# More sparse tiles at the end of a GroupNorm and patch top-k kernel, and dense stores that wait for sparse patches

## The reference, cut to what matters

```python
# x: (4, 256, 256, 256) float32
y = group_norm(x, groups=32)                     # (x - mean) / sqrt(var + 1e-5)
s = 0.5 * (|horizontal [-1,0,1] gradient of y| + |vertical gradient of y|) + 0.5 * |y|
sp = s averaged over patches of 32 x 32          # (4, 256 channels, 64 patches)
mask = rank of sp among the 256 channels < 128   # for each image and each patch position
out = x + y * mask
```

## Time and profile before

| | us |
|---|---|
| median of 3 runs (2054.36 to 2056.93) | 2055.26 |
| the profiled execution, its own time | 2053.4 |
| its span in the trace | 2051.6 |

### The profile page before, as it was taken

How to read it: one execution, slowest core, us unless ns; L and a number is a source line. 1 busy time by engine, 2 the same in 40 slices (tenths; PEclk the granted TensorE clock), 3 DMA queues, 4 the chain that set the end, 5 groups by cost and what they waited for, 6 DMA issues and landing times.

```text
span 2051.6 us, 16270 instructions
## 1 busy us (share of the span) xinstructions
PE 1373.3 (67%) x3528; PEld 674.0 (33%) x3528; DVE 1537.1 (75%) x2113; ACT 1593.2 (78%) x2405; POOL 1402.4 (68%) x975
## 2 busy tenths in 40 slices
PE   5899899786777777777767776877677777600000
PEld 2444444333333333433333333433333333300000
DVE  7988887888778787899787878888877787652210
ACT  4999999897898889998888898898888988730123
POOL 7999999677676667767766676767666766531226
PEclk9999999888988888988888888989888888855555
DMA  5898775199999999999999999999999999699995
GB/s 246 338 358 338 305 317 206 62 368 428 429 430 433 433 429 431 404 383 422 430 431 435 427 432 431 383 396 423 432 432 429 432 432 425 251 382 428 425 423 178
DMA packets 53672, 780.53 MB, mean 380 GB/s; under 512 B 11175, under 2 KB 11175, under 8 KB 16240
## 3 DMA queue, kind: packets, MB, share of 16 engines
q1 hardware_dynamic: 42096, 759.19, 88.1%
q0 software_dynamic: 11520, 20.77, 2.8%
HBM read 532.68 MB, written 293.60 MB: 403 GB/s over the span
## 4 chain that ended last, share of the span: by engine, by line
DMA 44%; ACT 16%; issue 11%; PE 8%; DVE 7%; another core or an unknown queue 6%; POOL 3%; DVEq 2%; SPq 1%; ACTq 1%; POOLq 0%
DMA again<-in_x_dram 41%; ACT again L706 8%; PE vertical L610 4%; PE vertical L612 4%; ACT thrown L764 3%; DVE stats L807 3%; DMA out_dram<-ring,pair 2%; DVEq L798 2%; ACT vertical L758 2%; ACT ring L724 1%; DVE largest L1000 1%; DMA ring<-in_x_dram 1%; SPq L464 1%; DVE vertical L821 1%
## 5 line engine op out<-in xcount | busy, mean ns | idle before, releaser
L610 PE MATMUL vertical<-ring,plus 128*128 128x512 f32 (+1 forms) x1200 | 667.1, 641 | 304.5 <-ACT vertical L758 304.0
L299 POOL TENSOR_TENSOR pair<-ring 128x960 f32<-128x960 f32 x360 | 638.2, 1793 | 30.5 <-DVE scratch L978 21.9
L612 PE MATMUL vertical<-ring,minus 128*128 128x512 f32 (+1 forms) x1200 | 633.3, 612 | 0.0
L807 DVE BATCH_NORM_STATS2 stats<-ring 128x6 f32<-128x512 f32 x960 | 582.2, 677 | 25.5 <-DMA ring<-in_x_dram 14.9
L764 ACT ACTIVATE thrown<-ring,record 128x1024 bf16<-128x1024 f32 x480 | 548.2, 1142 | 8.8
L706 ACT ACTIVATE again<-again,coef 128x1024 f32<-128x1024 f32 x360 | 416.1, 1227 | 165.7 <-DMA again<-in_x_dram 165.7
L834 DVE TENSOR_REDUCE sums<-pair 128x2 f32<-128x1920 f32 (+1 forms) x212 | 454.8, 2145 | 84.7 <-POOL pair L299 84.0
L305 POOL TENSOR_TENSOR pair<-ring 128x960 f32<-128x960 f32 x120 | 269.3, 2244 | 296.2 <-DVE sums L834 272.0
L610 PEld LDWEIGHTS vertical<-ring,plus 128*128 128x128 f32 x1200 | 240.7, 212 | 578.2 <-ACT vertical L758 364.9
L612 PEld LDWEIGHTS vertical<-ring,minus 128*128 128x128 f32 x1200 | 250.7, 209 | 296.2 <-issue 296.2
L758 ACT ACTIVATE vertical<-vertical 128x960 f32<-128x960 f32 x320 | 303.6, 949 | 24.7 <-PE vertical L612 24.7
(11 more groups left out here) (108 smaller groups left out, 1245.0 us busy)
## 6 DMA issues: line engine op xcount, KB each, us to landing
ring<-in_x_dram SPq DMA_DIRECT2D x59, 4096.0 KB, 23.3
again<-in_x_dram SPq DMA_DIRECT2D x98, 2048.0 KB, 15.5
out_dram<-again SPq DMA_DIRECT2D x98, 2048.0 KB, 14.9
out_dram<-kept SPq DMA_DIRECT2D x12, 2048.0 KB, 11.3
kept<-in_x_dram SPq DMA_DIRECT2D x4, 4096.0 KB, 23.5
out_dram<-ring SPq DMA_DIRECT2D x6, 2048.0 KB, 32.7
kept<-in_x_dram SPq DMA_DIRECT2D x4, 2048.0 KB, 26.5
ring<-in_x_dram SPq DMA_DIRECT2D x4, 2048.0 KB, 28.0
```

Source lines behind the costliest of these rows:

```text
L299: return nc.gpsimd.tensor_tensor(part.rearrange("p (r c) -> p r c", r=PATCH), xs[:, w, :, 2:], xs[:, w, :, 0:PATCH - 2], ALU.subtract)
L610: nc.tensor.matmul(v[:, first:end], plus[:], xs[:, first + 2 * PATCH:end + 2 * PATCH], start=True, stop=False)
L612: done = nc.tensor.matmul(v[:, first:end], minus[:], xs[:, first:end], start=False, stop=True)
L807: nc.vector.bn_stats(stats[:, k, :], buffer[:, k * BN:(k + 1) * BN])
```

## The change

Sparse tiles become 4 to 13 (ten) in place of 8 to 13 (six): five pairs instead of three. Dense halves become 12 (tiles 15, 14, 0 to 3) in place of 20. The loop of image 0 copies tiles 4 to 9 where it copied 8 to 13; tiles 10 to 13 are copied by four new calls, one behind each of the four `load_ahead` calls after the loop. Each dense store but the first has a second wait: store n is issued only after ACT has finished 6n sparse patch columns.

```diff
-SPARSE_FIRST, SPARSE_END = 8, LAST - 1
+SPARSE_FIRST, SPARSE_END = 4, LAST - 1
...
-assert SPARSE_PAIRS[0] == (LAST - RING, LAST - RING + 1) and SPARSE == 2 * (LOOPED - 2)
+
+SPARSE_PER_DENSE = 6
+assert SPARSE_PER_DENSE * (len(DENSE) - 1) < COLS * SPARSE
+assert SPARSE_PAIRS[0] == (LAST - RING, LAST - RING + 1) and SPARSE == 2 * (LOOPED - 2) + RING + 1
...
             for u in range(RING + 1):
                 load_ahead(0, LOOPED - 1, u)
+                copy_tile(base + SPARSE_END - RING - 1 + u)
...
             def store_dense(n):
                 t, half = DENSE[n]
                 sp.wait_ge(dense_finished, n + 1)
+                if n:
+                    sp.wait_ge(sparse_finished, SPARSE_PER_DENSE * n)
                 store_half(base + t, half, dense_slots[n % DENSE_SLOTS], dense_stored[n % DENSE_SLOTS])
```

## The result

The changed kernel takes 2037.93 us (median of 4 runs, 2037.54 to 2038.69) against 2055.22: a ratio of 0.9917, interval 0.9901 to 0.9933. That is 17.3 us less, where I had said 30 less (2025, range 2008 to 2041). The direction and the place were right; the size was 13 us off, and the time lies just outside the forecast's own spread (2013 to 2037).

What follows compares the result with a forecast made beforehand. The sparse chain on POOL, starved and then alone, was taken to set the end: 1992.8 without stalls + 19.2 stalls + 9.2 tail = span 2021.2, plus 3.7 = 2024.9, said as 2025 us, range 2008 to 2041.

Steps and rivals of the forecast that it cites:

- What bounds the stage: Last stage: the sparse chain on POOL sets the end, now starved for 190 us and then running alone.
- floor of 2002.0: Last stage: span if POOL issues without any stall until 1992.8, plus 9.2 us to the end.
- The copies in image 0 cost 0: End of image 0: four added copies are hidden by the loads' lead over DVE, 3.2 and 3.4 us left; cost 0.
- A dense half costs 5.5 us beside the sparse queue: Last stage: each dense transfer of 2.10 MB takes 5.5 us at 380 GB/s, sparse queue getting 47 GB/s.
- signs of being wrong: Last stage and image 1: gathers far from 47 GB/s beside a burst, first gathers well after 1832, or image 1 later.
- catch-up rate of 350 GB/s: Last stage: between dense bursts the sparse queue catches up at about 350 GB/s.
- The stalls: Last stage: POOL loses 4.0, 8.3, 0.5, 2.2 and 4.2 us to dense bursts and landings, 19.2 us in all.
- The tail: End of the last stage: 9.2 us from the end of the last scatter to the end of the span, unchanged.
- Rival (a): Last stage: POOL's pace alone, bursts cost nothing but the first 4 us; span 2006, time 2010; 14%.
- Rival (b): Last stage: bursts and sparse chain take turns, all 71.5 us; time 2081; slower than before from 64% of it; 10%.
- Rival (d): Last stage: the gate holds nothing back, dense work runs first; span 2065, time 2068; 2%.
- Rival (c): Last stage: DVE stops POOL for its whole length, 13 to 15 us more; time 2039; 6%.

Runs made afterwards that it cites:

- e3: Changed kernel with every dense store and load of the last stage left out, only the sparse chain left: span 2000.8 us, own time 2009.39 us.
- e6: Kernel before the change with four more copies alone, behind the loads at the end of image 0: 2053.95 us, ratio 1.000.
- e4: Changed kernel with only seven ungated dense stores left of the last stage, no sparse transfers: 5.1 us a half, 437 GB/s in mid-stream.
- e5: Changed kernel with only seven ungated dense stores and the first pair's 16 scatters left of the last stage: 6.2 us a half.
- e2: Kernel before the change with the gate alone, store n waiting for 2n sparse columns, six sparse tiles: 2045.44 us, ratio 0.996.
- e1: Changed kernel without the gate, ten sparse tiles, each dense store waiting for DVE alone: 2071.32 us, ratio 1.0078.
- e10: Changed kernel with the gate at 5n columns in place of 6n: 2036.55 us, ratio 0.9914.
- e11: Changed kernel with every dense transfer of the last stage cut in two by partitions (64 each), released 3 columns apart: 2082.58 us, ratio 1.0156.
- e12: Changed kernel with every dense transfer of the last stage cut in two by columns (8 KB rows), both parts at once: 2033.19 us, ratio 0.99.

## Why the prediction was right or wrong

- **What bounds the stage.** Right. With dense work left out the span is 2000.8, against my floor of 2002.0 and e3's own expectation of 2001. That it is so close has some luck in it: a later start (+1.4) and a shorter tail (-2.6) partly cancel, while POOL's 164.8 us are met to the tenth.
- **The copies in image 0 cost 0.** Right to within 2 us, by e6. In the changed kernel DVE read `kept` at 326.02 and tile 16 at 347.88, no later than before:

```profile
326.02 4.84 DVE L813 BATCH_NORM_STATS2 stats<-kept 128x6 f32<-128x512 f32 x8
...
347.88 2.46 DVE L813 BATCH_NORM_STATS2 stats<-ring 128x6 f32<-128x512 f32 x4
```

- **A dense half costs 5.5 us beside the sparse queue.** This is the term that was mis-sized. It came from a state in which the sparse queue moved only 47 GB/s beside an unbroken dense stream of 380. In the first bursts it measured 29.4 / 4 = 7.35 us, (1881.2 - 1854.9) / 4 = 6.6 and (1903.4 - 1888.5) / 2 = 7.45; alone it is 5.1 (e4), beside scatters 6.2 (e5). The sparse queue took more, 87 and 67 GB/s by the estimate above, and the sum of both queues was lower, 372 and 386 GB/s against some 427. That was one of the signs of being wrong that I had named. The catch-up rate of 350 GB/s was at most a little high (322 by e3, 344 by the page).
- **The stalls.** I listed 4.0, 8.3, 0.5, 2.2 and 4.2 us, 19.2 in all; the changed kernel had 34.8. The three large ones were in the right places: before the first gathers of pair 1 (4.0, measured 9.1), before its second tile's scatters (8.3, measured 13.7) and before the first gathers of pair 3 (4.2, measured 9.9). The two small ones of pair 2 (0.5 and 2.2) were not there; one of 2.2 came before its second gathers instead. The sum is 15.6 us too small. Each of the two longest ended with its dense burst, and four halves cost 7 us more than I had in the first and 4 in the second, so for this kernel the mechanism of the burst was right and its price was not. As a general account it is incomplete, since the gate at 7n moved the first stall without moving the burst.
- **The tail.** I kept 9.2 us; it was 2035.8 - 2029.2 = 6.6, 2.6 less. It is 9.2 again in e2 and e6, and 6.6 in e1, e3, e10, e11 and e12; why is open. **The start** came 1.6 us later. It scatters by more than that: in the profiled executions of all runs ACT starts between 1801.0 and 1805.2, and at 1802.4 in e6, which has copies too. Together: 15.6 - 2.6 + 1.6 = 14.6 us, the whole difference between the spans 2021.2 and 2035.8. In time it is 13.0, since the median lies 2.1 us above the profiled span and not 3.7.
- **Rival (a)**, POOL's pace alone (2010), didn't happen, but three buffers come within 6 us of it. **Rival (b)**, bursts and chain taking turns, happened in part: 30.8 us of 71.5 beyond (a)'s first 4 landed on the chain, 43%, where I had 21% and it turns slower at 64%. **Rival (d)**: the gate works; without one I had a span of 2065 and a time of 2068, and e1 measured 2065.9 in the profiled span and 2071 in time.
- **Rival (c), POOL beside DVE.** The measured 2037.9 is next to this rival's 2039, and that is chance: its 13 to 15 us are not in the trace. Beside the five loaded halves the slowest issues of POOL took 1.47 us (at 1883.6) and 1.43 (at 1838.8) in place of 0.96 to 1.05, and two at 1933.5 and 1934.9 took 1.05 and 1.13; with one at 1840.5 that is some 1.2 us in all. The gap of 2.2 us ended 0.2 us after DVE's half of 1903.4; the profile puts it down to the scatters' landing, and even counted whole it leaves the sum under 4 us. The Trainium skill ("SBUF — State Buffer", the warning on the "DVE blocks DMA" trap) says that GpSimd can't write descriptors while DVE runs an operation in a two-port mode. The trace doesn't name the mode, and one DVE instruction is only 2.98 / 4 = 0.745 us here, so a wait of one issue for the end of one instruction is not excluded. What did not hold is the reading of my rival, that POOL stands for the whole 14.9 us of DVE's work.

## What to carry to other kernels

Where two chains share the DMA engines and one of them is a long chain of small dependent transfers, hold the bulk stream back when you move work to that chain: here the move alone cost 0.8%, the hold alone gained 0.4%, and both together gained 0.8%. Then give the chain one more buffer, so that each landing has twice the issuing time as cover: that, with one load less in the first burst, gained another 1.0% (2016 us), more than the gate's step from 6n to 7n (0.6%), and brought the engines to 96% full. Try the gate at several values, since its effect was not smooth. Price a transfer from rows in which the other queue is as busy as it will be, not from rows in which it starved.

## What was not expected of the hardware

- Transfers of 64 partitions with rows of 16 KB, beside the sparse queue, kept the DMA engines full at 258 GB/s (e11, share 1.01); those of 128 partitions with the same rows reached 372 beside the sparse queue (the changed kernel's first burst, share 0.98) and 437 alone (e4).
- A batch of the sparse queue beside a dense burst does not land at a steady 47 GB/s. In the changed kernel the batches that POOL waited for landed 0.4 to 3.2 us after the end of dense work, and with the gate at 7n one landed 8 us before it. In the changed kernel both queues together moved 367 GB/s at a DMA share of 1.00 from 1829.6 to 1838.8; with stores and scatters alone it was 412 in mid-stream (e5).
- Halving the dense rows from 16 to 8 KB left the first stall as it was (9.2 against 9.1 us, e12).
